# Last three steps of an expert layer: the adds of the gathered expert sums move from GpSimd to VectorE, two of them into PSUM

## The chip, the cores and the metric

The kernel runs on one core of a Trainium2 chip. The metric is the device time of one execution in microseconds (us), lower is better. The engines are TensorE (PE in the profile, its weight loads PEld), VectorE (DVE), ScalarE (ACT), GpSimd (POOL) and SyncE (SP), which issues the DMA transfers spoken of here.

## The reference

Two layers run on an input x of 8 batches x 512 tokens x 256 features, each an attention-like part and a mixture of experts, each with a gated residual. The change is in the very last part, the experts of layer 1:

```
shared = silu(xt @ sg_w.T) * (xt @ su_w.T) @ sd_w.T        # every token
...
routed = einsum('te,teh->th', w, y)                        # two experts of eight for each token
h = layernorm(x) * (1 + cb) + sb
x = x + gb * (shared + routed)                             # gb: a row of 256 gates for each batch
```

So the output of each batch is x plus gate times the shared expert's product plus gate times the routed sum.

## The kernel before, in words

Matmuls are done in three passes of fp32r: every operand is split into a head (ScalarE, a rounding copy) and a rest (VectorE, operand minus head), and TensorE multiplies head x head, head x rest and rest x head. Nothing is scheduled automatically; each engine has its own instruction stream, written out by hand, and semaphores tie them.

The part is `silu_experts_part`. It has 47 steps. The first 5 are the shared expert on batches 0 to 4, then 39 tiles of 256 routed rows follow, and the last 3 steps are the shared expert on batches 5, 6 and 7; these three are called the first, second and third last step here. The routed tiles leave their rows by indirect DMAs that add into `sums_dram` in HBM (POOL queue, L2186). When all have landed (`added`), SP loads the sums back, 512 KB for each batch, into four buffers (L2151), and reloads a buffer when it was used (L2157). `ORDER` says which batch the n-th of these is.

A step on TensorE (`step`, L2212) is 8 products of 6 matmuls of 128x512 (gate and up, i = 0 to 3), and then a down product of 48 matmuls of 128x256, 12 for each i. It waits for `h_split` at its start (VectorE's rest of the step's input, `rest_of_h`, L2406), for `gu_done` from i = 2 on (the buffers of gate and up), and in the down product for `hidden_split` of each i (VectorE's rest of the hidden row, L2432).

VectorE's step is `products`: for each quarter i it multiplies silu(gate) by up from PSUM (`times_up`, L2424, 128x512) and takes the rest of the hidden row (L2432, 128x512), and at the end it takes the rest of the next step's input (L2406, 128x1024). `add_shared` (L2459, L2461) follows when the down product is done: the gate times PSUM, in place, then x plus that. In the second and third last steps each quarter also has one `gate_sums` (L2495, 128x1024): the gate times one batch's sums, in place. GpSimd then adds those sums to x (L2194), after `shared_added` for batches 5 and 6, and SP stores the batch (L2155). For batch 7 the sums are in x before its shared product; `add_last` works in two halves (L2505, L2511), and SP stores each half (L2161).

Of the kernel before, what the change touches and what calls it, by code (L numbers as in the profile page):

```python
# [17 lines left out]
ALU = mybir.AluOpType  # L18
# [4 lines left out]
B, S, D = 8, 512, 256  # L23
# [6 lines left out]
IC = F1 // P  # L30
# [1987 lines left out]
def silu_experts_part(c, ds, a, out):  # L2018
# [6 lines left out]
    nc = c.nc  # L2025
# [3 lines left out]
    BEFORE = 5  # L2029
    STEPS = B + TILES  # L2030
    LAST_SET = TILES + 1
    TILE_BASE = BEFORE * IC
    LAST_BASE = TILE_BASE + 2 * TILES
    N = B * NT
    with ExitStack() as ctx:
# [40 lines left out]
             "hidden_split down_done down_read shared_added gated summed tables_set counted listed turned "  # L2076
             "taken y_done added x_done stored").split())
        UNPACED = 6
        ORDER = [0, 1, 2, 3, 7, 4, 5, 6]

        def weights(buf, part):
            return w[:, buf, part].rearrange("p b c -> p (b c)")
# [10 lines left out]
        with nc.Block() as block:  # L2093
            @block.sync
            def _(sp):
# [55 lines left out]
                    sp.dma_start(sums[n], sums_view[ORDER[n]]).then_inc(sums_loaded[n], 16)  # L2151
                for n in range(B):
                    sp.wait_ge(summed, n + 1)
                    if ORDER[n] != B - 1:
                        sp.dma_start(view[ORDER[n]], c.x[:, ORDER[n]]).then_inc(stored, 16)  # L2155
                    if n + 4 < B:
                        sp.dma_start(sums[n % 4], sums_view[ORDER[n + 4]]).then_inc(sums_loaded[n % 4], 16)  # L2157
                for half in range(2):
                    sp.wait_ge(x_done, half + 1)
                    ts = slice(half * NT // 2, (half + 1) * NT // 2)  # L2160
                    sp.dma_start(view[B - 1, :, ts], c.x[:, B - 1, ts]).then_inc(stored, 16)  # L2161
                sp.wait_ge(stored, 16 * (B + 1))

            @block.gpsimd
            def _(pool):
                pool.iota(counts_i[:, 0:RUNGS], pattern=[[TS, RUNGS]], base=0, channel_multiplier=0)
                pool.iota(counts_i[:, RUNGS:RUNGS + TILES], pattern=[[1, TILES]], base=0, channel_multiplier=0)
                pool.iota(counts_i[:, RUNGS + TILES:], pattern=[[1, E]], base=0, channel_multiplier=0).then_inc(tables_set, 1)
                pool.wait_ge(tables_set, 1)
                nc.gpsimd.tensor_copy(ladder[:], counts_i[:, 0:RUNGS])  # L2170
                nc.gpsimd.tensor_copy(tile_numbers[:], counts_i[:, RUNGS:RUNGS + TILES])
                nc.gpsimd.tensor_copy(expert_numbers[:], counts_i[:, RUNGS + TILES:]).then_inc(tables_set, 1)
                LATE = 3
                for k in range(LATE * 2 * NT):
                    b = B - LATE + k // (2 * NT)
                    if k % (2 * NT) == 0:
                        ds.tag(pool, b)
                    if k >= UNPACED:
                        pool.wait_ge(hidden_split, k - UNPACED + 1)
                    ds.scatter(pool, b, k % (2 * NT))  # L2180
                for j in range(TILES):
                    pool.wait_ge(y_done, j + 1)
                    if j:
                        pool.wait_ge(added, 16 * TT * j)
                    for t in range(TT):
                        pool.indirect_dma_start(c.sums_dram[:, :],  # L2186
                                                bass.IndirectOffsetOnAxis(ap=row_ids[:, j % 2, t:t + 1], axis=0),
                                                y[:, j % 2, t, :], None, compute_op=ALU.add).then_inc(added, 16)
                for n in range(B):
                    b = ORDER[n]  # L2190
                    pool.wait_ge(gated, n + 1)
                    if BEFORE <= b < B - 1:
                        pool.wait_ge(shared_added, b + 1)
                    nc.gpsimd.tensor_tensor(c.x[:, b], c.x[:, b], sums[n % 4], ALU.add).then_inc(summed, 1)  # L2194

            @block.tensor
            def _(pe):
# [199 lines left out]
            def _(dve):  # L2397
# [14 lines left out]
                    nc.vector.tensor_tensor(h_parts[:, REST, :, cols], tp_ps[:, buf, :].rearrange("p (k s) -> p k s", k=KC),  # L2412
                                            h_parts[:, HEAD, :, cols].bitcast(F32), ALU.subtract).then_inc(h_split, 1)

                def products(n, base, next_h=None, next_set=None, sums_from=None):
                    def times_up(i):

                        if i < 2:
                            dve.wait_ge(down_read, n + 1)
                        else:  # L2420
                            dve.wait_ge(hidden_split, base + i - 1)
                        dve.wait_ge(silu_done, base + i + 1)
                        dve.wait_ge(up_done, base + i + 1)
                        nc.vector.tensor_tensor(gu[:, i % 2, :], silu[:, i % 2, :], up_ps[:, i % 2, :],  # L2424
                                                ALU.mult).then_inc(gu_done, 1)

                    times_up(0)
                    for i in range(IC):
                        if i + 1 < IC:
                            times_up(i + 1)  # L2430
                        dve.wait_ge(hidden_head_done, base + i + 1)
                        nc.vector.tensor_tensor(hidden[:, REST, i, :], gu[:, i % 2, :],  # L2432
                                                hidden[:, HEAD, i, :].bitcast(F32), ALU.subtract).then_inc(hidden_split, 1)
                        if next_set is not None and i < PARTS:
                            split_weight_rests(next_set, i, 1)
                        if sums_from is not None:
                            gate_sums(sums_from + i)
                    if next_h is not None:
                        rest_of_h(n + 1, next_h)

# [11 lines left out]
                                            hidden[:, HEAD, 2 * u:2 * u + 2, cols].bitcast(F32),  # L2452
                                            ALU.subtract).then_inc(hidden_split, 1)

                def add_shared(n, b):

                    dve.wait_ge(down_done, n + 2)
                    gate_row = c.gate[:, b, :].unsqueeze(1).broadcast_to([P, NT, D])
                    nc.vector.tensor_tensor(down_rows_ps, down_rows_ps, gate_row, ALU.mult)  # L2459
                    dve.drain()  # L2460
                    nc.vector.tensor_tensor(c.x[:, b], c.x[:, b], down_rows_ps, ALU.add).then_inc(shared_added, 1)  # L2461
                    dve.sem_inc(down_read, 1)
# [28 lines left out]
                def gate_sums(k):  # L2491

                    b, buf = ORDER[k], k % 4
                    dve.wait_ge(sums_loaded[buf], 16 * (k // 4 + 1))
                    nc.vector.tensor_tensor(sums[buf], sums[buf],  # L2495
                                            c.gate[:, b, :].unsqueeze(1).broadcast_to([P, NT, D]),
                                            ALU.mult).then_inc(gated, 1)

                def add_last():

                    dve.wait_ge(down_done, STEPS + 1)
                    dve.wait_ge(summed, ORDER.index(B - 1) + 1)
                    for half in range(2):
                        ts = slice(half * NT // 2, (half + 1) * NT // 2)
                        nc.vector.tensor_tensor(down_rows_ps[:, ts], down_rows_ps[:, ts],  # L2505
# [63 lines left out]
                tile_rest(TILES - 1, 0, 1)  # L2569
                split_weight_rests(LAST_SET, 2, 0)  # L2570
                rest_of_h(BEFORE + TILES, BEFORE)
                products(STEPS - 3, LAST_BASE, B - 2)
                add_shared(STEPS - 3, B - 3)
                products(STEPS - 2, LAST_BASE + IC, B - 1, sums_from=0)
                add_shared(STEPS - 2, B - 2)
                products(STEPS - 1, LAST_BASE + 2 * IC, None, sums_from=4)
                add_last()


# [88 lines left out]
```

## Time and profile before

| | before |
|---|---|
| median of 3 runs | 1655.76 us (1655.17 to 1656.09) |
| the profiled execution, its own time | 1656.67 us |
| its span in the trace | 1654.9 us |
| TensorE busy | 1495.6 us, 90% |
| VectorE busy | 1106.3 us, 67% |
| ScalarE busy | 899.0 us, 54% |
| GpSimd busy | 435.2 us, 26% |
| first last step starts on TensorE | 1588.38 us |

The profiled execution's own time is 1.8 us above its span. Busy shares are means over the whole kernel; the three last steps take some 67 us of it. In the page, PE is the matmul engine, DVE is VectorE, and a time behind `<-` is idle time with the engine that ended it.

### The profile page before, as it was taken

What the parts mean: (1) busy time and instruction counts of PE and PEld (TensorE: products, weight loads), DVE (VectorE), ACT (ScalarE), POOL (GpSimd) and SP (SyncE); (2) the same over time, 40 slices, a digit from 0 to 9 for tenths busy, and PEclk for the clock granted to TensorE, in tenths of its full rate; (3) what the DMA queues carried; (4) which work ended last, traced back from release to release, by engine and by line L of the source; (5) the groups of instructions that cost most, each with busy time, mean ns of one, the idle gap of its engine ahead of it and who ended that gap; (6) DMA issues with size and microseconds to landing.
All of it is one profiled execution on the core that took longest, in us unless ns stands there. A gap on an engine that the chain in (4) does not pass through costs nothing. (4 is left out here: it accounts for less than half of the span.)

```text
span 1654.9 us, 28864 instructions
## 1 busy us (share of the span) xinstructions
PE 1495.6 (90%) x10278; PEld 1152.0 (70%) x10278; DVE 1106.3 (67%) x2324; ACT 899.0 (54%) x1120; POOL 435.2 (26%) x421
## 2 busy tenths in 40 slices
PE   6899999968999978999999999876999999999996
PEld 4788888857888863344444444335889999999985
DVE  4577776578788873556566566255567777787757
ACT  2566655435555535555555555543347777777741
POOL 1122222230010131212214314213213333333324
PEclk9899999979999988999999999996999999999999
DMA  7000000210000000400000000005038888888844
GB/s 268 1 1 0 0 0 0 77 40 1 0 0 0 0 26 1 156 1 1 14 15 24 18 14 25 18 14 189 28 104 230 229 233 232 235 233 232 237 101 152
DMA packets 65454, 130.48 MB, mean 79 GB/s; under 512 B 8250, under 2 KB 38755, under 8 KB 64867
## 3 DMA queue, kind: packets, MB, share of 16 engines
q1 hardware_dynamic: 51074, 110.37, 21.1%
q0 software_dynamic: 14304, 19.15, 5.6%
q8 instruction: 42, 0.69, 0.2%
q14 instruction: 34, 0.27, 0.1%
HBM read 97.50 MB, written 32.00 MB: 78 GB/s over the span
## 5 line engine op out<-in xcount | busy, mean ns | idle before, releaser
L1760 ACT ACTIVATE at_wide<-at_sc_ps 128x2048 f32<-128x2048 f32 x128 | 240.5, 1879 | 173.5 <-PE at_sc_ps L1608 173.5
L2186 POOL DMA_INDIRECT sums<-e_y,e_row_ids x78 | 123.6, 1585 | 248.9 <-ACT e_y L2347 221.8
L1608 PE MATMUL at_sc_ps<-at_qT,at_kT 32*128 32x512 f32 x1024 | 151.7, 663 | 40.6 <-ACT at_wide L1760 38.1
L52 PE MATMUL e_gate_ps<-e_h_parts,e_w 128*128 128x256 f32 (+1 forms) x1128 | 176.8, 304 | 9.6 <-DVE e_h_parts L2406 3.7
L52 PE MATMUL e_up_ps<-e_h_parts,e_w 128*128 128x256 f32 (+1 forms) x1128 | 175.4, 303 | 0.0
L2401 DVE TENSOR_TENSOR e_w<-e_raw,e_w 128x1024 fp32r<-128x1024 f32 x123 | 147.0, 1222 | 41.4 <-ACT e_w L2300 40.6
L52 PEld LDWEIGHTS e_gate_ps<-e_h_parts,e_w 128*128 128x128 f32 x1128 | 155.1, 193 | 17.6 <-DVE e_h_parts L2406 4.1
L52 PEld LDWEIGHTS e_up_ps<-e_h_parts,e_w 128*128 128x128 f32 x1128 | 155.5, 193 | 7.9
L1622 PE MATMUL at_o_ps<-at_wide,at_v_ones 128*32 128x512 f32 x1024 | 139.1, 615 | 1.3 <-ACT at_wide L1760 1.3
L2257 PE MATMUL e_down_ps<-e_w,e_hidden 128*128 128x256 f32 x936 | 127.9, 286 | 2.2 <-DVE e_hidden L2450 2.2
L2300 ACT ACTIVATE e_w<-e_raw 128x1024 fp32r<-128x1024 f32 x123 | 125.3, 1048 | 5.7 <-DMA e_raw<-in_experts 5.7
L2257 PEld LDWEIGHTS e_down_ps<-e_w,e_hidden 128*128 128x128 f32 x936 | 117.4, 191 | 2.4 <-DVE e_hidden L2450 2.4
L52 PE MATMUL e_down_ps<-e_w_down,e_hidden 128*128 128x256 f32 x768 | 102.3, 283 | 8.3 <-DVE e_hidden L1132 7.9
L52 PEld LDWEIGHTS e_down_ps<-e_w_down,e_hidden 128*128 128x128 f32 x768 | 96.2, 189 | 17.7 <-DVE e_hidden L1132 8.3
L1143 DVE SCALAR_TENSOR_TENSOR e_acc<-e_down_ps,coef,e_acc 128x256 f32<-128x256 f32 x256 | 105.9, 475 | 2.7 <-PE e_down_ps L52 2.2
L52 PE MATMUL in_ps<-h_parts,w_in 128*128 128x512 f32 x384 | 100.8, 410 | 7.4 <-ACT hidden L602 4.6
L52 PE MATMUL e_up_ps<-e_h_parts,e_w_up 128*128 128x512 f32 x384 | 104.7, 409 | 2.0 <-DVE e_w_up L1177 2.0
L1608 PEld LDWEIGHTS at_sc_ps<-at_qT,at_kT 32*128 32x128 f32 x1024 | 41.4, 188 | 90.0 <-ACT at_wide L1760 53.2
L1363 POOL DMA_INDIRECT slots<-shared,ds_slots x64 | 70.2, 1096 | 123.0 <-DVE e_hidden L2432 57.3
L513 PE MATMUL out_ps<-w_out,hidden 128*128 128x256 f32 x768 | 99.3, 285 | 0.0
L513 PEld LDWEIGHTS out_ps<-w_out,hidden 128*128 128x128 f32 x768 | 95.8, 191 | 0.0
L52 PEld LDWEIGHTS in_ps<-h_parts,w_in 128*128 128x128 f32 x384 | 69.4, 191 | 37.0 <-ACT hidden L602 19.5
(348 smaller groups left out, 2638.1 us busy)
## 6 DMA issues: line engine op xcount, KB each, us to landing
e_raw<-in_experts SPq DMA_DIRECT2D x123, 512.0 KB
e_rows_in<-slots SPq DMA_DIRECT2D x39, 272.0 KB
sums<-shared SPq DMA_DIRECT2D x17, 256.0 KB
x<-in_L_attn_x SPq DMA_DIRECT2D x8, 512.0 KB, 9.6
gate<-gates SPq DMA_DIRECT2D x4, 1024.0 KB
slots<-shared SPq DMA_DIRECT2D x15, 272.0 KB
out<-x SPq DMA_DIRECT2D x7, 512.0 KB, 3.1
e_sums<-sums SPq DMA_DIRECT2D x4, 512.0 KB, 4.4
```

What stands on the lines that cost most here:

```text
L52: last = pe.matmul(out, left(i), right(j), start=n == 0, stop=n == len(steps) - 1)
L513: last = nc.tensor.matmul(to, hidden[:, i, m, cols], w_out[:, j, m, :], start=False, stop=m == MC - 1 and n == 2)
L1143: last = nc.vector.scalar_tensor_tensor(out=acc[:, t, :], in0=rows_of(down_ps[e % 2], t), scalar=c.coef[:, b, t, e:e + 1], in1=acc[:, t, : ...
L1363: pool.indirect_dma_start(self.c.slots_dram, bass.IndirectOffsetOnAxis(ap=self.slots[:, which, at:at + 1], axis=0), self.rows[:, b % 2, t, ...
L1608: last = nc.tensor.matmul(sc_ps[:, m, :], kT[strip, par, quad % 2, quad // 2, k * P:(k + 1) * P], qT[strip, par, quad // 2, :], start=True ...
L1622: last = nc.tensor.matmul(o_ps[MW * m:MW * (m + 1), quad % 2, :], v_ones[:, par, k, at:at + MW], wide[:, u % 2, m * S:(m + 1) * S], start= ...
L1760: nc.scalar.activation(wide[:, u % 2, :], sc_ps[:].rearrange("p n s -> p (n s)"), ACT.Sigmoid, scale=float(HD) ** -0.5).then_inc(sig_done, 1)
L2186: pool.indirect_dma_start(c.sums_dram[:, :], bass.IndirectOffsetOnAxis(ap=row_ids[:, j % 2, t:t + 1], axis=0), y[:, j % 2, t, :], None, co ...
L2257: last = nc.tensor.matmul(down_ps[:, buf, t * D:(t + 1) * D], hidden[:, p, i, at:at + P], down_rows(1 - buf, r, i), start=i == 0 and m == ...
L2300: nc.scalar.activation(w[:, buf, HEAD, q], raw[:, q], ACT.Copy).then_inc(w_head_done, 1)
L2401: nc.vector.tensor_tensor(w[:, buf, REST, q], raw[:, q], w[:, buf, HEAD, q].bitcast(F32), ALU.subtract).then_inc(w_split, 1)
```

## The change

The eight adds of the sums leave GpSimd. For batches 0, 1, 2, 3, 4 and 7 VectorE does both operations, gate times sums and x plus that (`gate_sums`, `add_sums`), alternately, one behind each quarter of a step, from the third quarter of the first last step on; the pair of batch 7 stands ahead of `add_last`. For batches 5 and 6 `add_shared` first adds the sums to the down product in PSUM, and the gating and the add to x that were there serve both. `ORDER` follows, and SP now reloads a buffer first and stores x after that, with a wait for `shared_added`.

```diff
-        ORDER = [0, 1, 2, 3, 7, 4, 5, 6]
+        GATED = {0: 1, 2: 2, 3: 3, 5: 4, 6: 5, 7: 6}
+        ORDER = [0, 5, 1, 2, 6, 3, 4, 7]
...
                 for n in range(B):
                     sp.wait_ge(summed, n + 1)
-                    if ORDER[n] != B - 1:
-                        sp.dma_start(view[ORDER[n]], c.x[:, ORDER[n]]).then_inc(stored, 16)
                     if n + 4 < B:
                         sp.dma_start(sums[n % 4], sums_view[ORDER[n + 4]]).then_inc(sums_loaded[n % 4], 16)
+                    if ORDER[n] != B - 1:
+                        sp.wait_ge(shared_added, ORDER[n] + 1)
+                        sp.dma_start(view[ORDER[n]], c.x[:, ORDER[n]]).then_inc(stored, 16)
...
-                for n in range(B):
-                    b = ORDER[n]
-                    pool.wait_ge(gated, n + 1)
-                    if BEFORE <= b < B - 1:
-                        pool.wait_ge(shared_added, b + 1)
-                    nc.gpsimd.tensor_tensor(c.x[:, b], c.x[:, b], sums[n % 4], ALU.add).then_inc(summed, 1)
...
-                def add_shared(n, b):
+                def add_shared(n, b, with_sums=False):
 
                     dve.wait_ge(down_done, n + 2)
+                    if with_sums:
+                        k = ORDER.index(b)
+                        dve.wait_ge(sums_loaded[k % 4], 16 * (k // 4 + 1))
+                        nc.vector.tensor_tensor(down_rows_ps, down_rows_ps, sums[k % 4], ALU.add).then_inc(summed, 1)
+                        dve.drain()
...
+                def add_sums(k):
+                    dve.wait_ge(gated, GATED[k])
+                    nc.vector.tensor_tensor(c.x[:, ORDER[k]], c.x[:, ORDER[k]], sums[k % 4], ALU.add).then_inc(summed, 1)
+
+                def beside_first(i):
+                    if i == 2:
+                        gate_sums(0)
+                    elif i == 3:
+                        add_sums(0)
+
+                def beside_second(i):
+                    if i % 2 == 0:
+                        gate_sums(2 + i // 2)
+                    else:
+                        add_sums(2 + i // 2)
+
+                def beside_third(i):
+                    if i % 2 == 0:
+                        gate_sums(5 + i // 2)
+                    else:
+                        add_sums(5 + i // 2)
+
                 def add_last():
 
+                    gate_sums(B - 1)
+                    add_sums(B - 1)
                     dve.wait_ge(down_done, STEPS + 1)
-                    dve.wait_ge(summed, ORDER.index(B - 1) + 1)
+                    dve.wait_ge(summed, B)
...
-                products(STEPS - 3, LAST_BASE, B - 2)
-                add_shared(STEPS - 3, B - 3)
-                products(STEPS - 2, LAST_BASE + IC, B - 1, sums_from=0)
-                add_shared(STEPS - 2, B - 2)
-                products(STEPS - 1, LAST_BASE + 2 * IC, None, sums_from=4)
+                products(STEPS - 3, LAST_BASE, B - 2, sums_beside=beside_first)
+                add_shared(STEPS - 3, B - 3, with_sums=True)
+                products(STEPS - 2, LAST_BASE + IC, B - 1, sums_beside=beside_second)
+                add_shared(STEPS - 2, B - 2, with_sums=True)
+                products(STEPS - 1, LAST_BASE + 2 * IC, None, sums_beside=beside_third)
```

VectorE before, from the first last step's fourth `times_up` to the end of its `add_shared` (`e_sums` and `shared` are the four buffers of sums):

```order
L2424 TENSOR_TENSOR e_gu_silu<-e_gu_silu,e_up_ps 128x512
L2432 TENSOR_TENSOR e_hidden<-e_gu_silu,e_hidden 128x512 x2
L2406 TENSOR_TENSOR e_h_parts<-hT,e_h_parts 128x1024
L2459 TENSOR_TENSOR e_down_ps<-e_down_ps,gate 128x1024
L2461 TENSOR_TENSOR x<-x,e_down_ps 128x1024
```

The same place in the changed kernel:

```order
L2420 TENSOR_TENSOR e_gu_silu<-e_gu_silu,e_up_ps 128x512
L2428 TENSOR_TENSOR e_hidden<-e_gu_silu,e_hidden 128x512
L2496 TENSOR_TENSOR e_sums<-e_sums,gate 128x1024
L2428 TENSOR_TENSOR e_hidden<-e_gu_silu,e_hidden 128x512
L2502 TENSOR_TENSOR x<-x,e_sums 128x1024
L2402 TENSOR_TENSOR e_h_parts<-hT,e_h_parts 128x1024
L2457 TENSOR_TENSOR e_down_ps<-e_down_ps,e_sums 128x1024
L2460 TENSOR_TENSOR e_down_ps<-e_down_ps,gate 128x1024
L2462 TENSOR_TENSOR x<-x,e_down_ps 128x1024
```

Two operations of 128x1024 now stand ahead of the rest of the next step's input, and the add in PSUM stands ahead of the gating.

VectorE before, from the third last step's fourth `times_up` to the end of the kernel:

```order
L2424 TENSOR_TENSOR e_gu_silu<-e_gu_silu,e_up_ps 128x512
L2432 TENSOR_TENSOR e_hidden<-e_gu_silu,e_hidden 128x512
L2495 TENSOR_TENSOR shared<-shared,gate 128x1024
L2432 TENSOR_TENSOR e_hidden<-e_gu_silu,e_hidden 128x512
L2495 TENSOR_TENSOR shared<-shared,gate 128x1024
L2505 TENSOR_TENSOR e_down_ps<-e_down_ps,gate 128x512 x2
L2511 TENSOR_TENSOR x<-x,e_down_ps 128x512 x2
```

The same place in the changed kernel:

```order
L2420 TENSOR_TENSOR e_gu_silu<-e_gu_silu,e_up_ps 128x512
L2428 TENSOR_TENSOR e_hidden<-e_gu_silu,e_hidden 128x512
L2496 TENSOR_TENSOR shared<-shared,gate 128x1024
L2428 TENSOR_TENSOR e_hidden<-e_gu_silu,e_hidden 128x512
L2502 TENSOR_TENSOR x<-x,shared 128x1024
L2496 TENSOR_TENSOR shared<-shared,gate 128x1024
L2502 TENSOR_TENSOR x<-x,shared 128x1024
L2530 TENSOR_TENSOR e_down_ps<-e_down_ps,gate 128x512 x2
L2536 TENSOR_TENSOR x<-x,e_down_ps 128x512 x2
```

Two more operations of 128x1024 stand between the last rest and the gating of the last down product.

## Rows read from the trace of the kernel before

**Rows 1.** The page: busy us (share of the span) xinstructions.

```profile
PE 1495.6 (90%) x10278; PEld 1152.0 (70%) x10278; DVE 1106.3 (67%) x2324; ACT 899.0 (54%) x1120; POOL 435.2 (26%) x421
```

**Rows 2.** Stretches of the first and second last step: us, busy of each engine, clock, DMA.

```profile
1588.30:1605.30 17.00, 16.92 (x97) 15.03 (x98) 6.49 (x10) 5.64 (x10) 3.12 (x2) 1.00 0.52 143
1605.30:1626.70 21.40, 17.17 (x97) 14.66 (x95) 18.63 (x16) 5.53 (x9) 8.59 (x4) 1.00 0.37 118
```

**Rows 3.** TensorE in order of time: start us, us, line, operation [idle before].

```profile
1616.05 3.03 PE L2229 MATMUL e_down_ps<-e_w,e_hidden 128*128 128x256 f32 x24
1620.58 3.42 PE L2229 MATMUL e_down_ps<-e_w,e_hidden 128*128 128x256 f32 x24 [1.50 <-DVE e_hidden L2432]
1626.77 1.65 PE L52 MATMUL e_gate_ps<-e_h_parts,e_w 128*128 128x512 f32 x6 [2.76 <-DVE e_h_parts L2406]
...
1642.29 3.44 PE L2229 MATMUL e_down_ps<-e_w,e_hidden 128*128 128x256 f32 x24 [1.48 <-DVE e_hidden L2432]
```

**Rows 4.** The chain that ended last, in order of time: start us, us.

```profile
1599.56 5.75 PE e_down_ps L2229 x48
1605.31 1.39 PE e_gate_ps L52 x6
1606.69 1.36 PE e_up_ps L52 x6
```

**Rows 5.** VectorE around the end of the first last step.

```profile
1600.30 1.47 DVE L2432 TENSOR_TENSOR e_hidden<-e_gu_silu,e_hidden 128x512 fp32r<-128x512 f32 x2
...
1605.35 1.23 DVE L2459 TENSOR_TENSOR e_down_ps<-e_down_ps,gate 128x1024 f32<-128x1024 f32 x1 [2.10 <-PE e_down_ps L2229]
1606.65 1.22 DVE L2461 TENSOR_TENSOR x<-x,e_down_ps 128x1024 f32<-128x1024 f32 x1
1608.20 0.69 DVE L2424 TENSOR_TENSOR e_gu_silu<-e_gu_silu,e_up_ps 128x512 f32<-128x512 f32 x1 [0.32 <-PE e_up_ps L52]
```

**Rows 6.** VectorE in the second last step.

```profile
1613.63 0.69 DVE L2424 TENSOR_TENSOR e_gu_silu<-e_gu_silu,e_up_ps 128x512 f32<-128x512 f32 x1 [0.30 <-PE e_up_ps L52]
1614.24 2.14 DVE L2432 TENSOR_TENSOR e_hidden<-e_gu_silu,e_hidden 128x512 fp32r<-128x512 f32 x1
...
1617.43 0.68 DVE L2424 TENSOR_TENSOR e_gu_silu<-e_gu_silu,e_up_ps 128x512 f32<-128x512 f32 x1
1618.03 2.49 DVE L2432 TENSOR_TENSOR e_hidden<-e_gu_silu,e_hidden 128x512 fp32r<-128x512 f32 x1
...
1622.19 3.39 DVE L2495 TENSOR_TENSOR shared<-shared,gate 128x1024 f32<-128x1024 f32 x1
1625.50 1.21 DVE L2406 TENSOR_TENSOR e_h_parts<-hT,e_h_parts 128x1024 fp32r<-128x1024 f32 x1
```

**Rows 7.** GpSimd in the second last step.

```profile
1613.42 2.40 POOL L2194 TENSOR_TENSOR x<-x,e_sums 128x1024 f32<-128x1024 f32 x1 [20.02 <-DVE e_sums L2495]
1617.59 2.38 POOL L2194 TENSOR_TENSOR x<-x,e_sums 128x1024 f32<-128x1024 f32 x1 [1.76 <-DVE e_sums L2495]
```

**Rows 8.** VectorE at the end of the kernel.

```profile
1647.22 1.28 DVE L2505 TENSOR_TENSOR e_down_ps<-e_down_ps,gate 128x512 f32<-128x512 f32 x2
1648.42 1.27 DVE L2511 TENSOR_TENSOR x<-x,e_down_ps 128x512 f32<-128x512 f32 x2
```

**Rows 9.** The first loads of sums: issue ns, first and last start; issue to landing.

```profile
L2151 SPq DMA_DIRECT2D e_sums<-sums x2: 383/446/508, 1595.6 to 1596.0; - x2
...
DMA to landing us min/median/max: 3.9/5.3/6.4
```

**Rows 10.** The stores of whole batches, in the same columns.

```profile
L2155 SPq DMA_DIRECT2D out<-x x7: 372/378/383, 1615.9 to 1649.8; - x7
...
DMA to landing us min/median/max: 2.9/3.1/3.2
```

**Rows 11.** The stores of batch 7's halves, in the same columns.

```profile
L2161 SPq DMA_DIRECT2D out<-x x2: 507/750/994, 1650.2 to 1650.7; - x2
...
DMA to landing us min/median/max: 3.3/3.4/3.5
```

**Rows 12.** One microsecond of the end, columns as in rows 2.

```profile
1651.00:1652.00 1.00, 0.00 (x0) 0.00 (x0) 0.00 (x0) 0.00 (x0) 0.00 (x0) 0.50 1.04 345
```

More of the change, by code:

```diff
@@ L2413, in rest_of_rows, with products @@
                                             h_parts[:, HEAD, :, cols].bitcast(F32), ALU.subtract).then_inc(h_split, 1)
-                def products(n, base, next_h=None, next_set=None, sums_from=None):
+                def products(n, base, next_h=None, next_set=None, sums_beside=None):
                     def times_up(i):
@@ L2435, in products @@
                             split_weight_rests(next_set, i, 1)
-                        if sums_from is not None:
-                            gate_sums(sums_from + i)
+                        if sums_beside is not None:
+                            sums_beside(i)
                     if next_h is not None:
```

## The prediction

> **What bounds the kernel now.** I read the page first: TensorE is busy 90% of the span, the others far less [rows 1]. Nothing ahead of the first last step changes (the instructions of every engine are the same up to there), so the answer lies in the last 67 us. Next the stretches: in the first last step TensorE is busy 16.92 of 17.00 us and VectorE 6.49; in the second the step takes 21.40 us, TensorE is busy for only 17.17 of them, and VectorE for 18.63 [rows 2]. Then TensorE in order of time: in the second last step it stands still for 1.50 us amid the down product, for VectorE's rest of the hidden row, and for 2.76 us ahead of the third, for VectorE's rest of the input; in the third for 1.48 us amid the down product [rows 3]. So in these two steps VectorE sets the pace. The chain gives the pace of a step without such waits: 1.39 for its first product, 7 times 1.36, and 5.75 for the down product, 16.66 us [rows 4].
>
> Why VectorE is late is in its rows. A rest of 128x512 takes 1.47 us for two alone (0.6 apart), but 2.14 and 2.49 us where a GpSimd add runs [rows 5, 6]. GpSimd's second add runs from 1617.59 to 1619.97; VectorE's rest starts at 1618.03 and ends at 1620.52, 0.55 us behind the add's end, which is about its own work. The first add ends at 1615.82 and the rest beside it at 1616.38, again 0.56 later. The gating at 1622.19 takes 3.39 where such an operation takes 1.21 [rows 6, 7]. The product at 1617.43, one input of which is PSUM, is not stretched: 0.68 with the add running from 1617.59 on. I read this as: a VectorE operation with both inputs in SBUF does not advance while a GpSimd add does. The excess of one step is (2.14 - 0.68) + (2.49 - 0.68) + (3.39 - 1.21) = 5.45 us.
>
> **The change part by part.** *GpSimd.* Its adds are gone, and with them the 5.45 us of each of the two steps.
>
> *VectorE's work.* Before: 8 gatings. After: 6 gatings, 6 adds, 2 adds in PSUM, so 6 operations more. Gatings and SBUF adds are priced as the input rest, 1.21 us busy and 1.15 from start to start (a first end overlaps the next start by 0.07) [rows 6]. The trace has no add of SBUF sums onto PSUM; the nearest row is L2459, the same shape, PSUM in and out, 1.23 and 1.30 to the next with the drain between [rows 5]. Its bounds are 1.15 (as if SBUF) and 1.30; I take 1.30.
>
> *First last step, by VectorE's stream.* The third rest starts at 1600.30 [rows 5]. Gating of batch 0 at 1600.90, if its sums are there: the first load was issued at 1595.6, and the shortest landing is 3.9 us, so 1599.5 [rows 9]. The fourth rest from 1602.04, ending 1602.7; TensorE wants it three quarters into the down product, 1599.56 + 4.31 = 1603.87 [rows 4]. Add from 1602.64, input rest from 1603.79 to 1605.00; TensorE wants it at 1605.31. It fits with 0.3 us to spare, less 0.06 for the semaphore: cost 0. Bounds: 0, and 0.9 us if the four loads share the queues so that the first lands as late as the last (issued some 1.5 us later, 6.4 us to landing, about 1603) less what is spare; in between for the median, 5.3. I take 0, since the shortest landing must be somebody's and the first is the likely one.
>
> *Second last step.* `add_shared` starts at 1605.35 as before, and has three operations: 1605.35, 1606.65, 1607.95, ending at 1609.2. The first product then starts 1.0 us later than its 1608.20 [rows 5]. Behind it waits TensorE's third gate product, due two product pairs after 1605.31, hence at 1605.31 + 1.39 + 3 x 1.36 = 1610.78, and 1609.2 + 0.7 = 1609.9 is in time. From there: gating 1612.1 to 1613.3 (as before), product at 1613.63 [rows 6], rest 1614.24 (now 0.68), add 1614.84 to 1616.05, product at 1616.35 (2.72 behind the last, with up's product), rest 1616.95, gating 1617.55, rest 1618.70 to 1619.38 (TensorE wants it at 1616.2 + 4.3 = 1620.5), add 1619.30, input rest 1620.45 to 1621.66. TensorE ends the down product at 1605.31 + 16.66 = 1621.97. Neither wait is left: the third last step starts at 1621.97 in place of 1626.77 [rows 3]. **Gain 4.80 us.**
>
> *Third last step.* The same calculation, 16.66 later: three operations of `add_shared` to 1625.8, product to 1626.5 (due 1627.4), and no wait of TensorE. Its end falls at 1638.63, 16.66 behind the start, where it was 1642.29 + 3.44 - 1626.77 = 18.96 [rows 3]. **Gain 2.30.**
>
> *Ahead of the last adds.* Before, TensorE ended at 1645.73 and VectorE went on at 1647.22 [rows 3, 8], 1.49 later. Now: third product 1630.3, rest 1630.9, add 1631.5, fourth product 1633.0, rest 1633.6, gating 1634.2, rest 1635.35, add 1635.95, gating 1637.1, add 1638.25 to 1639.47. That is 0.85 behind TensorE's end. Here VectorE is the bound. **Gain 0.64.** The four half operations are unchanged, 1647.22 to 1649.69 [rows 8], now to 1641.95.
>
> *The tail.* Before, from the last add to the span's end 5.2 us: the whole store of the last batch goes out ahead of the halves, at 1649.8, since GpSimd's last add was as late [rows 10]; the halves follow at 1650.2 and 1650.7 and land 3.3 to 3.5 us later, about 1654.0, and the span ends 0.85 behind that [rows 11]. Now the last whole store is issued at about 1637.2 and has landed by 1640.4. The second half's store starts at about 1642.0 behind a first half of 256 KB alone. A lone store of 256 KB is not in the trace: 512 KB take 2.9 to 3.2, of which 1.52 is moving at 345 GB/s [rows 10, 12], so 256 KB should take 2.9 - 0.76 = 2.15 to 2.45; the upper bound is 3.3, as before. I take 2.3: landing 1644.3, end 1645.15, 3.2 behind the last add. **Gain 2.0**, at least 1.0.
>
> The Trainium skill, DMA: Bandwidth & Descriptors, section "Anatomy of one DMA — SWDGE (gpsimd) path", gives a DMA about 2 us of fixed cost. The rows make it 1.4 to 1.7 for these stores; an estimate by the page, 2.0 + 0.76 = 2.8, would make the gain of the tail 1.5 in place of 2.0, and the sum 0.5 less.
>
> *Sum.* 4.80 + 2.30 + 0.64 + 2.0 = 9.7 us. I take off 0.1 for waits of VectorE on its own semaphore where an add stands right behind its gating. The profiled execution's 1656.67 (span 1654.9 and 1.8 around it) becomes 1647.1. Its time is 0.9 above the median of the runs; the median becomes 1655.76 - 9.6 = **1646.2**.
>
> **The rivals.** *1. VectorE too full: it becomes the bound.* Cover is 0.3 us in the first last step, and VectorE is already 0.85 behind at the end. Late sums (0.9, above), operations 0.1 us dearer than priced where each waits for a semaphore (14 of them, 1.4 us), a tail of 3.3 (1.0): each of these leaves 6.5 to 8.6 us of gain, 1647.2 to 1649.3. For it: the margins. Against it: all prices are rows of the same shapes.
>
> *2. The stretched rows are not GpSimd's doing.* Then VectorE keeps its 5.45 us. In the second step two gatings and two adds stand where four gatings stood: no change. In the third, three of each and none of the waits gone: 2 x 1.15 more, less the 2.0 of the tail, 1656.1: no change to measure. Against it: two ends that both fall 0.55 us behind a GpSimd add's end [rows 6, 7].
>
> That is also where a page would speak against the change. The Trainium skill, Perfetto Trace Analysis, section "Optimizing Scalar/DVE Operations", says that with a full VectorE moving work to another engine, even GpSimd, may make sense, and warns that the two share a port of SBUF. By the first half of that sentence, taking 6 operations back costs 7 us of VectorE and gives rival 2 or worse; by the second half, the stretched rows are the price of sharing. The trace is on the side of the second.
>
> *3. Slower: the first gating waits for its sums.* It stands ahead of the fourth rest and of the input rest, so behind it wait TensorE's down product and its next step. From 1600.9 on, less 0.25 us, each microsecond of a later landing is one of TensorE. The gain is used up with a landing at 1610.8, and 0.2% are lost (3.3 us) from 1614.1 on, against 1599.5 [rows 9]. Before, this wait had 12 us of slack (the first gating was at 1612.1), so a late landing would not have shown. Against it: the loads are issued at 1595.6 and the longest landing is 6.4.
>
> **How the numbers follow.** Forecast 0.77, with its own range 1645.3 to 1647.6 (1.0 less in the tail, 0.4 of waits; 0.9 better if the last gating overlaps more than I have it); rival 1 0.17; rival 2 0.05; rival 3 0.01. The range 1645.2 to 1649.2 takes in rival 1. What a measurement of this kernel tells from no change is about 0.2%, 3.3 us. Faster by more than that: 0.94; within it 0.05; slower 0.01.
>
> **What would show it.** In the profile after: no GpSimd row behind the indirect DMAs; every 128x512 rest at 0.68 and every 128x1024 operation at 1.2; the three last steps starting 16.7 apart on TensorE, at about 1588.4, 1605.3 and 1622.0, with no idle time for L2428 or L2402; the last VectorE row ending near 1642; the span near 1645.2. The prediction is wrong if rests stay at 2 us (rival 2), if TensorE waits ahead of the second last step for VectorE (rivals 1 and 3), or if the last VectorE operation ends more than 1.5 us behind TensorE's last.

## The result and the profile after

The changed kernel took 1643.35 us (median of 4 runs, 1642.25 to 1644.69) against 1655.92 us, a ratio of 0.9922 with a 95% interval of 0.9909 to 0.9934. It is faster, as forecast, but by 12.6 us where 9.6 were forecast, and outside the stated range (1645.2 at its low end). The profiled execution took 1642.25 us, its span is 1640.5 us.

The page and three stretches of the profile after, one for each last step (us, busy of each engine, clock, DMA share, GB/s), answer to [rows 1, 2]:

```profile
PE 1488.7 (91%) x10278; PEld 1150.0 (70%) x10278; DVE 1104.4 (67%) x2330; ACT 899.3 (55%) x1120; POOL 414.4 (25%) x413
```

```profile
1583.90:1600.70 16.80, 16.78 (x97) 14.89 (x98) 8.56 (x11) 5.58 (x10) 3.12 (x2) 1.00 0.53 142
1600.70:1617.40 16.70, 16.70 (x99) 14.80 (x98) 14.36 (x16) 5.54 (x9) 0.00 (x0) 1.00 0.56 188
1617.40:1634.20 16.80, 16.80 (x97) 14.68 (x96) 14.72 (x17) 4.58 (x8) 0.00 (x0) 1.00 0.40 134
```

TensorE is busy throughout, and each step takes 16.7 to 16.8 us. In the second of them VectorE does 16 operations, as many as in that stretch before, and is busy for 14.36 us where it was 18.63.

TensorE in order of time after, for [rows 3]:

```profile
1583.92 1.65 PE L52 MATMUL e_gate_ps<-e_h_parts,e_w 128*128 128x512 f32 x6 [0.93 <-DVE e_h_parts L2402]
...
1600.68 1.56 PE L52 MATMUL e_gate_ps<-e_h_parts,e_w 128*128 128x512 f32 x6
...
1611.60 5.92 PE L2225 MATMUL e_down_ps<-e_w,e_hidden 128*128 128x256 f32 x48
1617.36 1.55 PE L52 MATMUL e_gate_ps<-e_h_parts,e_w 128*128 128x512 f32 x6
...
1628.28 5.91 PE L2225 MATMUL e_down_ps<-e_w,e_hidden 128*128 128x256 f32 x48
```

The down products are one piece of 48, and no step but the first has an idle time ahead of it. But look at the first row: the first last step starts at 1583.92, where it was 1588.38. No engine's instructions ahead of that point differ between the two kernels. So 4.46 us of the 14.4 us between the two spans come from a stretch that the change doesn't touch. Some 1.1 us of it is a single wait of TensorE in the last routed tile of the profile before, where VectorE had waited 1.18 us for one of the DMAs that add into the sums (the row of VectorE at 1582.10); the other seventeen profiles of this record have 1.04 or 1.05 us at this place:

```profile
1585.76 1.70 PE L2257 MATMUL e_down_ps<-e_w,e_hidden 128*128 128x256 f32 x12 [2.17 <-DVE e_hidden L2450]
```

From that start to the span's end it is 66.52 us before and 56.58 after: 9.94 us.

VectorE after, in the second last step and at the end (for [rows 6, 8]), then the last pair of stores (for [rows 11]):

```profile
1614.24 0.69 DVE L2428 TENSOR_TENSOR e_hidden<-e_gu_silu,e_hidden 128x512 fp32r<-128x512 f32 x1
1614.85 1.22 DVE L2502 TENSOR_TENSOR x<-x,shared 128x1024 f32<-128x1024 f32 x1
1615.98 1.22 DVE L2402 TENSOR_TENSOR e_h_parts<-hT,e_h_parts 128x1024 fp32r<-128x1024 f32 x1
1617.56 1.23 DVE L2457 TENSOR_TENSOR e_down_ps<-e_down_ps,e_sums 128x1024 f32<-128x1024 f32 x1 [0.36 <-PE e_down_ps L2225]
...
1632.66 1.22 DVE L2496 TENSOR_TENSOR shared<-shared,gate 128x1024 f32<-128x1024 f32 x1
1633.91 1.22 DVE L2502 TENSOR_TENSOR x<-x,shared 128x1024 f32<-128x1024 f32 x1
1635.24 1.30 DVE L2530 TENSOR_TENSOR e_down_ps<-e_down_ps,gate 128x512 f32<-128x512 f32 x2
1636.45 1.27 DVE L2536 TENSOR_TENSOR x<-x,e_down_ps 128x512 f32<-128x512 f32 x2
```

```profile
L2163 SPq DMA_DIRECT2D out<-x x2: 373/373/373, 1637.2 to 1637.8; - x2
...
DMA to landing us min/median/max: 2.2/2.3/2.4
```

Every rest is back at 0.68 or 0.69 us, the add in PSUM takes 1.23, and the rest of the input ends at 1617.20, where the third last step starts at 1617.36, so there is little to spare. The last adds begin 1.05 us behind TensorE's end (1634.19), and the lone stores of 256 KB land in 2.2 to 2.4 us.

### The profile page after: what moved, and what is told of

It reads as the page before. It is cut to its first block and busy times, and to the rows that moved or that the text cites. A ratio compares the mean times of both kernels' runs of the same rounds, so it can differ in the third digit from the quotient of the medians.

```text
span 1640.5 us, 28867 instructions
## 1 busy us (share of the span) xinstructions
PE 1488.7 (91%) x10278; PEld 1150.0 (70%) x10278; DVE 1104.4 (67%) x2330; ACT 899.3 (55%) x1120; POOL 414.4 (25%) x413
## 5 line engine op out<-in xcount | busy, mean ns | idle before, releaser
L52 PEld LDWEIGHTS e_gate_ps<-e_h_parts,e_w 128*128 128x128 f32 x1128 | 155.3, 193 | 14.4 <-DVE e_w L2397 3.2
```

The lines of the kernel that those rows point to most:

```text
L52: last = pe.matmul(out, left(i), right(j), start=n == 0, stop=n == len(steps) - 1)
```

## The experiments

**The same kernels again.** Both kernels, unchanged, to see what belongs to a kernel and what to an execution.

> The kernel before, unchanged. The changed kernel's profile starts its first last step at 1583.9 us where before it was 1588.4: 4.5 us of the gain lie ahead of any instruction that the change touches, and the last part by itself gave 9.9. Theory 1 (chance of an execution): this copy lies within 1.5 us of the kernel before in its median, but its profile may start the first last step anywhere from 1584 to 1589. Theory 2 (it belongs to the built kernel): 1655.9 within 0.5 us, and the first last step again at 1588 to 1589.

> The changed kernel, unchanged. Theory 1: over more executions its median rises towards 1655.9 less the 9.9 us of the last part, 1646.0, and the first last step starts anywhere from 1584 to 1589. Theory 2: 1643.3 within 0.7 us, and the first last step at 1584 to 1585 again. In both, from the first last step's start to the span's end 56.6 us.

The kernel before: median 1657.2 us in 11 executions as this copy, 1654.73 in 15 beside it, one and the same program, 1653.55 to 1659.0 in all. The changed kernel: 1644.44 (1643.35 to 1645.17), ratio 0.9932 (0.9918 to 0.9946). The profiles start the first last step at 1585.94 and 1586.12, and the changed kernel's stretch to the end is 56.58 again (1642.7 less 1586.12). So theory 1 holds for what lies ahead: where the first last step starts belongs to the execution. The two first profiles lay at or near its two ends by chance. Neither theory has the medians right: this copy's lies 2.5 us above that of the same program beside it, where 1.5 was the most expected, and the changed kernel's did not rise to 1646.0.

But the copy of before held something not expected: 68.16 us from the first last step's start to the end (1654.1 less 1585.94), not 66.52. TensorE in the copy's third last step, and the granted clock there (second fence, columns as above):

```profile
1624.35 2.77 PE L52 MATMUL e_gate_ps<-e_h_parts,e_w 128*128 128x512 f32 x6 [2.76 <-DVE e_h_parts L2406]
1626.93 2.04 PE L52 MATMUL e_up_ps<-e_h_parts,e_w 128*128 128x512 f32 x6
1628.80 1.53 PE L52 MATMUL e_gate_ps<-e_h_parts,e_w 128*128 128x512 f32 x6
```

```profile
1623.00:1627.00 4.00, 2.65 (x7) 2.06 (x8) 3.66 (x4) 0.00 (x0) 3.29 (x1) 0.69 0.84 262
```

The same six matmuls took 1.65 us in [rows 3]. Behind the wait of 2.76 us the clock is granted at 1.2 GHz for some microseconds (0.69 is a mean of the two levels over the 4 us), and the step takes 20.56 us where it took 18.96.

**GpSimd's adds left out.** The kernel before without them; VectorE's stream is as it was. The routed sums never reach x.

```diff
-                for n in range(B):
-                    b = ORDER[n]
-                    pool.wait_ge(gated, n + 1)
...
-                    nc.gpsimd.tensor_tensor(c.x[:, b], c.x[:, b], sums[n % 4], ALU.add).then_inc(summed, 1)
...
-                    sp.wait_ge(summed, n + 1)
+                    sp.wait_ge(gated, n + 1)
```

> The kernel before without GpSimd's eight adds; VectorE's stream is untouched, and the routed sums never reach x. My theory (an operation with both inputs in SBUF stands while a GpSimd add runs): every 128x512 rest at 0.68 us and every gating at 1.21, no wait of TensorE in the last two steps, last add 1.0 us sooner than in the changed kernel behind TensorE, 10.5 us gained from the first last step on (56.0 us from its start to the end of the span). Rival (the stretch has another cause in VectorE's own stream): the rests keep 2.1 to 2.5 us, TensorE keeps its waits of 1.5 and 2.8 us, and only the last stores are sooner, 2 us.

1642.74 us, ratio 0.9922 (0.9908 to 0.9935), 55.5 us from the first last step's start (1586.08) to the end (1641.6). VectorE in its second last step:

```profile
1614.67 0.69 DVE L2428 TENSOR_TENSOR e_hidden<-e_gu_silu,e_hidden 128x512 fp32r<-128x512 f32 x1
1615.27 1.22 DVE L2491 TENSOR_TENSOR shared<-shared,gate 128x1024 f32<-128x1024 f32 x1
1616.41 0.69 DVE L2428 TENSOR_TENSOR e_hidden<-e_gu_silu,e_hidden 128x512 fp32r<-128x512 f32 x1
1617.01 1.22 DVE L2491 TENSOR_TENSOR shared<-shared,gate 128x1024 f32<-128x1024 f32 x1
1618.14 1.22 DVE L2402 TENSOR_TENSOR e_h_parts<-hT,e_h_parts 128x1024 fp32r<-128x1024 f32 x1
```

The same instructions as in [rows 6], with nothing beside them on GpSimd, and none is stretched. Nor does TensorE wait in the last two steps. The stretched rows are GpSimd's doing. The rival falls.

**The adds back on GpSimd, in the changed order.** Six adds; those in PSUM stay on VectorE.

```diff
+                for k in GATED:
+                    pool.wait_ge(gated, GATED[k])
+                    pool.wait_ge(summed, k)
+                    nc.gpsimd.tensor_tensor(c.x[:, ORDER[k]], c.x[:, ORDER[k]], sums[k % 4], ALU.add).then_inc(summed, 1)
...
                 def add_sums(k):
-                    dve.wait_ge(gated, GATED[k])
-                    nc.vector.tensor_tensor(c.x[:, ORDER[k]], c.x[:, ORDER[k]], sums[k % 4], ALU.add).then_inc(summed, 1)
+                    pass
```

> The changed kernel, in its order, with the two adds in PSUM, but the six adds to x done by GpSimd again. My theory: a rest or an input rest beside each add is stretched again, up to 2.5 us in place of 0.68; with two adds in a step in place of four the second last step loses 0.4 to 1.5 us, the first up to 0.9, and in all it is 1 to 3 us slower than the changed kernel. Rival (spreading and PSUM made the gain, not the engine): equal to the changed kernel within 0.5 us.

1647.77 us, ratio 0.9952 (0.9939 to 0.9966), 3.3 us above the changed kernel beside it; from the first last step's start to the end 61.1 us in place of 56.6, 4.5 more. The expectation had 1 to 3, so this is dearer than expected by either measure. One GpSimd add and the VectorE rest beside it:

```profile
1598.74 2.78 POOL L2194 TENSOR_TENSOR x<-x,e_sums 128x1024 f32<-128x1024 f32 x1 [10.10 <-DVE e_sums L2501]
```

```profile
1599.18 3.43 DVE L2406 TENSOR_TENSOR e_h_parts<-hT,e_h_parts 128x1024 fp32r<-128x1024 f32 x1
```

The input rest ends 1.09 us behind the add's end (1601.52), which is about its own work: it makes no headway until the add is done. Here the operation beside the add is the one that TensorE waits for, so it stood still 0.81 us ahead of the second last step and 0.88 ahead of the third, and the last pair ran one behind the other on two engines: the last adds began at 1640.74, 3.3 us behind TensorE's end.

**A wait put in, and two.** The changed kernel, with operations of VectorE that nobody needs, so that TensorE stands still as it did before.

```diff
-                products(STEPS - 2, LAST_BASE + IC, B - 1, sums_beside=beside_second)
+                products(STEPS - 2, LAST_BASE + IC, None, sums_beside=beside_second)
+                for m in range(3):
+                    cols = slice(0, 512 if m == 2 else 1024)
...
+                    dve.drain()
+                rest_of_h(STEPS - 1, B - 1)
```

> The changed kernel with three operations of VectorE that nobody needs ahead of the input rest of the third last step, so that TensorE waits there for about 2.8 us as it did before; nothing else is changed. The wait by itself makes it 2.8 to 3.3 us slower than the changed kernel. Theory of the clock: in some of the executions 1.6 us more than that, so that the median is 3 to 5 us above and the executions spread over 4 us or more. Rival (no second price): 2.8 to 3.3 above, in the spread of the changed kernel (2 to 3 us).

1647.09 us (1646.16 to 1648.08), ratio 0.9949 (0.9936 to 0.9962), 3.1 above the changed kernel's 1644.0 over all its executions; TensorE's wait was 3.11 us and the stretch from the first last step's start to the end 60.0 us, 3.4 more:

```profile
1622.12 1.66 PE L52 MATMUL e_gate_ps<-e_h_parts,e_w 128*128 128x512 f32 x6 [3.11 <-DVE e_h_parts L2402]
```

No second price, and a spread of 1.9 us: a miss for the theory in this form. What the kernel before has besides is another wait shortly ahead, 1.50 us in the down product. So both were put in, the other by three such operations behind the second quarter:

```diff
                 def beside_second(i):
+                    if i == 1:
+                        idle_for_others(3, 1024)
```

> The changed kernel with idle time for TensorE put into the second last step in two places, as it was before: three unneeded operations of VectorE ahead of the fourth product, so that the down product waits some 1.5 to 2.5 us, and three ahead of the input rest, so that the third last step starts 2.8 to 3.1 us late. Theory (one wait of 3.1 us left the clock alone; it is both waits together that cost the clock, as in two of the three profiles of the kernel before): TensorE's granted clock falls to 1.2 GHz at the start of the third last step, which gets 1.6 us longer than 16.66; the median is 6 to 8 us above the changed kernel, the waits alone 4.5 to 5.7. Rival (the fall in the kernel before has to do with GpSimd or with nothing here): the step takes 16.9 us as in the run with one wait.

1653.65 us (1651.34 to 1654.29, 9 executions), ratio 0.9979 (0.9969 to 0.9989), 9.8 above the changed kernel beside it, where 6 to 8 were expected. The first wait was 2.12 us, within what was meant, the second came out longer, 3.94; the stretch is 65.7 us, 9.1 above the changed kernel. TensorE behind the two waits:

```profile
1617.53 3.44 PE L2225 MATMUL e_down_ps<-e_w,e_hidden 128*128 128x256 f32 x24 [2.12 <-DVE e_hidden L2428]
1624.90 2.93 PE L52 MATMUL e_gate_ps<-e_h_parts,e_w 128*128 128x512 f32 x6 [3.94 <-DVE e_h_parts L2402]
```

The clock fell, and this step ran 19.2 us from its start to TensorE's last matmul, where a step started from rest runs 16.9. So VectorE's lateness alone brings it about, without GpSimd. Whether it takes two waits is not shown here, since the second is also longer than the single one of 3.11 us; for two speaks the kernel before, whose longest wait is 2.76. These times lie in two groups, 1651.3 to 1652.2 and 1653.7 to 1654.3.

**Sooner.** The changed kernel with one operation on the sums behind the first product of each of the last two steps, where VectorE stands idle for TensorE, and none ahead of the last adds.

```diff
                     times_up(0)
+                    if sums_beside is not None:
+                        sums_beside(-1)
...
+                SECOND = {-1: (gate_sums, 2), 0: (add_sums, 2), 1: (gate_sums, 3), 2: (add_sums, 3), 3: (gate_sums, 5)}
+                THIRD = {-1: (add_sums, 5), 0: (gate_sums, 6), 1: (add_sums, 6), 2: (gate_sums, 7), 3: (add_sums, 7)}
```

> The changed kernel with the operations on the sums begun one place sooner in the last two steps: one behind the first product, where VectorE stands idle for 1.1 to 1.5 us for TensorE, and so none left ahead of the last adds. Theory (VectorE's last pair is the bound by 1.0 us, all else TensorE): last adds 0.05 us behind TensorE's end in place of 1.0 to 1.1, 55.5 us from the first last step's start to the span's end in place of 56.6, 1.0 us faster. Rival (the tail of stores is the bound): no change.

> The changed kernel again, beside the next one: 56.6 us from the first last step's start to the span's end, 1642 to 1646 us in all.

> The kernel with the operations begun one place sooner, again, beside the changed kernel on the same chip: 55.6 us from the first last step's start to the span's end, so 1.0 us less; in whole times 0.5 to 1.5 us less, if the executions' own spread of 2 to 4 us lets it be seen.

The profiles give 55.57 and 55.60 us (1641.6 less 1586.03, 1643.2 less 1587.60) against 56.58, 56.58 and 56.61 for the changed kernel: 1.0 us, as worked out. The last adds wait for TensorE now:

```profile
1636.34 1.30 DVE L2531 TENSOR_TENSOR e_down_ps<-e_down_ps,gate 128x512 f32<-128x512 f32 x2 [1.49 <-PE e_down_ps L2225]
```

In whole times 1643.26 (ratio 0.9927, 0.9915 to 0.9939) and, beside the changed kernel's 1643.86 (0.9924, 0.9911 to 0.9938), 1642.39 (0.9913, 0.9900 to 0.9927). The executions of the two kernels overlap: the 1.0 us is shown by the stretch, and not by whole times.

**Every add right behind its gating.** The kernel before with VectorE doing the adds, two operations behind each quarter, none in PSUM, none in the first last step.

```diff
+                    dve.wait_ge(gated, k + 1)
+                    if BEFORE <= b < B - 1:
+                        dve.wait_ge(shared_added, b + 1)
+                    nc.vector.tensor_tensor(c.x[:, b], c.x[:, b], sums[buf], ALU.add).then_inc(summed, 1)
```

> The kernel before with every add moved from GpSimd to VectorE right behind its gating, in the old order: none in PSUM, none in the first last step, two operations behind each quarter. Theory (the engine is one half, spreading and PSUM are the other): VectorE has 8 x 1.15 in each of two steps and is the bound; TensorE waits some 2 us in the down product and some 2 us ahead of the third last step, 62.7 us from the first last step's start to the span's end, 5 to 6 us slower than the changed kernel and 3 to 4 us faster than before. Rival (taking the adds off GpSimd is all): equal to the changed kernel within 1 us.

1649.99 us, ratio 0.9965 (0.9953 to 0.9978), 6 us above the changed kernel's 1644.0; its stretch is 64.1 us. TensorE waits for VectorE:

```profile
1618.58 1.69 PE L2223 MATMUL e_down_ps<-e_w,e_hidden 128*128 128x256 f32 x12 [1.30 <-DVE e_hidden L2426]
1622.11 2.05 PE L52 MATMUL e_gate_ps<-e_h_parts,e_w 128*128 128x512 f32 x6 [1.84 <-DVE e_h_parts L2400]
```

So moving the adds to another engine, by itself, is a third to a half of the gain: 4.1 of 11.6 us by the stretches (68.15 less 64.1), 5.6 of 11.8 by the medians. The stretch is 1.4 us longer than expected: the clock fell here too (2.05 us for these six matmuls, 2.75 for the next).

**Nothing in the first last step.** The changed kernel with batch 0's pair moved into the second.

```diff
-        ORDER = [0, 5, 1, 2, 6, 3, 4, 7]
+        ORDER = [5, 0, 1, 2, 6, 3, 4, 7]
...
+                    for op, k in {0: [(gate_sums, 1)], 1: [(add_sums, 1)], 2: [(gate_sums, 2), (gate_sums, 3)],
+                                  3: [(add_sums, 2), (add_sums, 3)]}[i]:
+                        op(k)
```

> The changed kernel without its two operations in the first last step: batch 0's pair goes into the second, which then has six operations in its four quarters. Theory (VectorE has about 0.3 us to spare in the second last step, and each operation costs 1.15): the input rest ends 2.0 us behind TensorE's down product, the third last step starts 2.0 to 2.3 us late, and the rest of the kernel is as in the changed one: 58.6 to 58.9 us from the first last step's start to the end in place of 56.6. Rival (VectorE has room enough): 56.6.

1645.71 us, ratio 0.9940 (0.9927 to 0.9954); 58.8 us from the first last step's start to the end, as expected, with TensorE idle for 1.71 us ahead of the third last step. Two operations of 1.15 us past what fits cost 2.2 us by the stretch, 1.9 by whole times. The clock did not fall behind this wait.

**How often the clock falls in the kernel before.** Single profiles.

> The kernel before once more, for its profile alone. In the last copy TensorE's clock was granted at 1.2 GHz for some microseconds right behind the 2.76 us wait ahead of the third last step, and that step took 1.6 us longer than in the profile before. Theory (the wait sometimes costs more than itself, by the clock): from the first last step's start to the span's end either 66.5 us (clock stays at 2.4 GHz) or 68.2 us (it falls), nothing between. Rival (that execution was disturbed otherwise): 66.5 us.

> The kernel before, one profile. If the clock's fall behind the wait accounts for the 1.6 us, the stretch from the first last step's start to the span's end is 68.2 us in most of these three profiles and 66.5 us in the rest, and never between; if it was chance in two profiles, 66.5 us in most.

> As same_before3: 68.2 or 66.5 us, with or without a granted clock of 1.2 GHz at the start of the third last step.

> As same_before3: 68.2 or 66.5 us, with or without a granted clock of 1.2 GHz at the start of the third last step.

> The changed kernel with both waits put in, one profile. From the first last step's start to the end 65.7 us with the clock fallen (as in the last profile) or about 63.4 us without; a time between speaks against the clock as the cause of the two groups.

The stretch from the first last step's start to the span's end, in the order of the copies: 68.15, 69.4, 68.1 and 68.2 us, with the first copy's 68.16 and the first profile's 66.52. In each of the five the granted clock fell to 1.2 GHz around the start of the third last step, between 0.7 us ahead of it and 0.6 us behind it; in the first profile it did not fall, though TensorE's waits are the same to 0.01 us. The one of 69.4 lay in neither group that was expected; there the low clock lasted into the third product, which took 1.94 us:

```profile
1625.81 2.93 PE L52 MATMUL e_gate_ps<-e_h_parts,e_w 128*128 128x512 f32 x6 [2.76 <-DVE e_h_parts L2406]
1628.54 2.76 PE L52 MATMUL e_up_ps<-e_h_parts,e_w 128*128 128x512 f32 x6
1631.10 1.94 PE L52 MATMUL e_gate_ps<-e_h_parts,e_w 128*128 128x512 f32 x6
```

The kernel with two waits gave 65.15 us (1649.9 less 1584.75), with the fall as well. Both its profiles are of the lower group of times, so what sets its upper group is not seen.

## Why the prediction was right and wrong

*The mechanism* was right in what it named, and left out TensorE's clock. The stretched rows were GpSimd's (no_pool_adds, pool_back), and the rule of the Trainium skill, Perfetto Trace Analysis, "Optimizing Scalar/DVE Operations", that offloading between these two engines might not help, is what the traces here show: six adds on GpSimd cost 3.3 us more than on VectorE by the medians, 4.5 by the stretches.

*The first and second last step*: with the 4.46 us added, each row of VectorE lies within 0.15 us of where it was put, but for the second last step's first gating, 0.4 later. First start to second 16.76, second to third 16.68 (forecast 16.66). The cover in the first last step held; the gating of batch 0 did not wait for its sums.

*Ahead of the last adds*: 0.85 forecast, 1.05 measured. *The tail*: 3.2 forecast from the last add to the span's end, 2.8 measured (1637.72 to 1640.5). The lone store lands in 2.2 to 2.4, which bears out the rows' 1.4 to 1.7 beside the transfer. The estimate by the 2 us of the Trainium skill, DMA: Bandwidth & Descriptors, "Anatomy of one DMA — SWDGE (gpsimd) path", was 2.8; that section is on transfers that GpSimd issues, these stores are issued by SyncE, and the measurement decides.

*The sum* from the first last step on: 9.7 forecast, 9.94 measured between the two profiles. By terms, that is 4.94 for the second last step (4.80 forecast), 2.13 for the third (2.30), 0.44 ahead of the last adds (0.64) and 2.43 for the tail (2.0). The third is smaller since the forecast set 16.66, from start to start, against 18.96, from start to TensorE's end; from start to end it is 16.83 after. The whole time moved by more, and the step that failed is this term: "*Third last step.* The same calculation, 16.66 later ... Its end falls at 1638.63, 16.66 behind the start, where it was 1642.29 + 3.44 - 1626.77 = 18.96. Gain 2.30." The 18.96 us are right for the profile that was shown. In five further profiles of the same kernel that step takes 20.5 to 20.6 us, once 21.8, since TensorE's clock falls behind the waits; no profile of the changed kernel has the waits or the fall. By the forecast's own calculation the term is 3.8 to 3.9, once 5.2, and not 2.3, in five profiles of six. I priced TensorE's waits at their length and had no row on what they do to the clock.

*From the profile to the median*: the prediction subtracted the gain of one profile from a median of three runs, and allowed for nothing that differs between executions ahead of the first last step. It starts at 1588.38 in the profile before, and at 1583.65 to 1587.40 in the other five of the same kernel; in the changed kernel's three at 1583.92 to 1586.19. One part of it goes with the clock again. The stretch from 340 to 370 us in the profile before, then in the copy whose first last step starts soonest:

```profile
340.00:370.00 30.00, 23.57 (x110) 18.36 (x111) 19.57 (x43) 15.90 (x23) 13.06 (x18) 0.74 0.19 55
```

```profile
340.00:370.00 30.00, 22.75 (x122) 18.10 (x123) 22.43 (x48) 16.09 (x23) 14.37 (x18) 0.85 0.20 56
```

Over both kernels, the three profiles with a granted clock of 0.84 or 0.85 in this stretch start their first last step at 1583.65 to 1584.60, the six with 0.69 to 0.75 at 1585.94 or later.

With all executions taken together the kernel before has a median of 1655.8 us (60, 1653.4 to 1659.0) and the changed one 1644.0 us (14, 1642.25 to 1645.17): 11.8 us. From the first last step on the medians of the profiles give 68.15 - 56.58 = 11.6. So 11.6 of the 11.8 us lie where the change is; of the first comparison's 12.6, about 0.8 was the draw of executions. The draw alone does not explain the miss: 1644.0 lies below the range as well. The range's low end should have been lower by the 1.6 us of the clock and about 1 us for the draw.

*The rivals.* Rival 1 (VectorE too full) did not come; no_first and dve_behind show that it was near, 2.2 us for two operations. Rival 2 fell. Rival 3 did not come. None of them was in the direction in which the time went: nothing in the list made the change better than the sum.

What stays open: why one profile in six keeps its clock, whether one wait of 3.1 us never costs it (one profile, and five times within 1.9 us), and whether it is two waits close together or their length that does.

## What to carry to other kernels

A VectorE operation with both inputs in SBUF stood still here while GpSimd added in SBUF; so an add of 2.4 us "for nothing" on GpSimd held a VectorE operation beside it for 1.5 to 2.2 us, where the same add on VectorE costs 1.15. Where VectorE sets the pace, take the work back and put it, one operation at a time, where VectorE waits for TensorE. Where TensorE waits twice within a few microseconds, look whether the granted clock falls behind the waits, and price them with that; and read a gain from a stretch that both kernels run, with some executions of each: whole times of one program here differed by 5.6 us.

## What was not expected

TensorE's granted clock fell to 1.2 GHz behind waits of 1.50 and 2.76 us, 6.2 us from the end of one to the end of the other, in five profiles of six, at a cost of 1.6 us and once 2.9 us; behind waits of 0.35, 1.30 and 1.84 us in dve_behind; and not behind a single one of 3.11 in stall_put. A GpSimd add takes 2.78 us in place of 2.40 where VectorE's rest (1598.57 in pool_back) had begun ahead of it: the two stand for each other both ways. The trace before shows it already, in its second last step, where rows of VectorE had begun at 1621.59 and 1625.50:

```profile
1621.74 2.76 POOL L2194 TENSOR_TENSOR x<-x,shared 128x1024 f32<-128x1024 f32 x1 [1.77 <-DVE shared L2495]
1625.66 3.31 POOL L2194 TENSOR_TENSOR x<-x,shared 128x1024 f32<-128x1024 f32 x1 [1.16 <-DVE shared L2495]
```
